# Stored parts in places of their own, a written order for TensorE, and four extra matmuls

## What is computed

```python
Q, K = rope(x @ qw), rope(x @ kw)                 # 16 heads of 8
score = einsum('bhqd,bhkd->bhqk', Q, K) / sqrt(8) - 1e10 * (1 - causal)
weights = softmax(score - max(score))
attn = einsum('bhqk,bhkd->bhqd', weights, V)
x = layernorm(x + merged(attn) @ ow)
gates = top-2 of softmax(x @ router_w + router_b), normalised
h = silu(x @ w1[e]) * (x @ w3[e])
x = layernorm(x + sum_e gates[e] * (h @ w2[e]))
```

## Time and profile before

| what | us |
|---|---|
| median of three runs | 496.91 (495.39 to 498.34) |
| the profiled execution, its time | 497.89 |
| its span, first to last instruction | 496.2 |
| TensorE busy | 416.2 |
| VectorE busy | 313.3 |
| ScalarE busy | 267.1 |
| GpSimd busy | 190.2 |

### The profile page before, as it was taken

One profiled execution on the slowest core, in us unless ns is written; L12 is line 12 of the kernel. 1 busy time (PEld: TensorE's weight loads), 2 busy tenths in 40 slices (PEclk: granted clock), 3 DMA queues, 4 the chain that ended last, 5 costly groups with the idle time before them and its releaser, 6 DMA issues.

```text
span 496.2 us, 7475 instructions
## 1 busy us (share of the span) xinstructions
PE 416.2 (84%) x2397; PEld 209.4 (42%) x2420; DVE 313.3 (63%) x1027; ACT 267.1 (54%) x377; POOL 190.2 (38%) x255
## 2 busy tenths in 40 slices
PE   5715473899898998989989888989999999999992
PEld 2302310222223222232222322327888788788781
DVE  3526374687887878878778786333556756765844
ACT  1220300557556576575755757676665575565560
POOL 3631320205215152151431513224565574665662
PEclk9957555799999999999999999889999999999996
DMA  6644544021122121221212100000000000000000
GB/s 230 190 125 120 159 100 122 13 63 47 20 65 50 47 61 24 65 49 40 60 33 64 41 3 0 3 0 1 2 0 2 21 1 1 22 1 2 22 0 21
DMA packets 46198, 23.47 MB, mean 47 GB/s; under 512 B 30320, under 2 KB 43248, under 8 KB 46160
## 3 DMA queue, kind: packets, MB, share of 16 engines
q1 hardware_dynamic: 46160, 23.00, 17.6%
HBM read 14.21 MB, written 8.59 MB: 46 GB/s over the span
## 4 chain that ended last, share of the span: by engine, by line
PE 58%; DVE 17%; SPq 7%; DMA 6%; ACT 5%; issue 4%; POOL 2%; POOLq 0%; DVEq 0%; ACTq 0%
PE o_bank L1055 12%; PE t_bank L1123 8%; PE bank L1123 8%; PE t_bank L1134 8%; DVE maxima L789 7%; PE t_bank L1038 6%; PE bank L1015 6%; PE small_bank L1015 3%; DMA q_op<-max_rows 3%; SPq L408 3%; DVE mg_w L785 2%; DVE mg_t L785 2%; DVE x_w L785 2%; SPq L367 2%; ACT num L628 2%
## 5 line engine op out<-in xcount | busy, mean ns | idle before, releaser
L628 ACT ACTIVATE num<-t_bank 128x1024 f32<-128x1024 f32 (+2 forms) x160 | 145.1, 939 | 110.1 <-PE t_bank L1038 108.8
L549 POOL TENSOR_TENSOR hid_lo<-num,q_op 128x512 fp32r<-128x512 f32 x64 | 83.0, 1300 | 60.9 <-ACT q_op L684 59.7
L518 POOL TENSOR_SCALAR_AFFINE_SELECT num<-num 128x512 f32<-128x512 f32 x64 | 40.3, 636 | 145.6 <-ACT num L628 145.5
L1015 PE MATMUL bank<-k_op,q_op 128*128 128x512 bf16 (+7 forms) x241 | 74.4, 338 | 22.8 <-DMA k_op<-k_scratch 10.8
L1055 PE MATMUL o_bank<-num,v_op 128*32 128x512 f32 (+3 forms) x768 | 84.5, 513 | 1.1
L1038 PE MATMUL t_bank<-q_op,k_op 64*128 64x512 bf16 (+3 forms) x384 | 59.8, 339 | 11.9 <-DMA q_op<-max_rows 10.2
L684 ACT ACTIVATE q_op<-num 128x512 fp32r<-128x512 f32 x64 | 40.5, 632 | 45.1 <-DVE num L916 44.7
L789 DVE TENSOR_REDUCE maxima<-bank 128x1 f32<-128x512 f32 x85 | 58.4, 688 | 7.9 <-PE bank L1015 4.5
L785 DVE CUSTOM_DVE_ANT_0 mg_t<-bank,resid 128x320 f32<-128x320 f32 (+6 forms) x85 | 37.9, 446 | 23.2 <-PE bank L1015 14.4
L1015 PEld LDWEIGHTS bank<-k_op,q_op 128*128 128x128 bf16 x255 | 23.2, 98 | 67.3 <-DVE maxima L789 20.8
L1038 PEld LDWEIGHTS t_bank<-q_op,k_op 64*128 64x128 bf16 x384 | 16.0, 93 | 76.6 <-issue 46.3
(11 more groups left out here) (132 smaller groups left out, 640.8 us busy)
## 6 DMA issues: line engine op xcount, KB each, us to landing
k_op<-k_scratch SPq DMA_DIRECT2D x32, 128.0 KB, 2.3
q_op<-q_scratch SPq DMA_DIRECT2D x64, 51.0 KB
q_scratch<-rope_part SPq DMA_DIRECT2D x24, 128.0 KB, 2.4
k_scratch<-rope_part SPq DMA_DIRECT2D x24, 128.0 KB, 2.4
w_raw<-in_w_all SPq DMA_DIRECT2D x6, 512.0 KB, 4.1
xT<-in_x_feat SPq DMA_DIRECT2D x4, 256.0 KB, 5.4
k_scratch<-k_op SPq DMA_DIRECT2D x4, 256.0 KB
q_op<-max_rows SPq DMA_DIRECT2D x64, 3.0 KB
```

Source lines behind the costliest of these rows:

```text
L518: pool.affine_select(out=tile, in_=tile, compare_op=ALU.is_ge, fill=0.0, base=0, pattern=[[0, GH], [1, P]], channel_multiplier=-1)\
L549: pool.tensor_tensor(hid_lo[:, m % HB, :], hid[:, m % HB, :], hid_hi[:, m % HB, :].bitcast(F32), ALU.subtract).then_inc(f_lo, 1)
L628: act.activation(num[:, t % PB, :, off:CH].rearrange("p (k i) t -> p i k t", i=2)[:, :, h:h + each, :], t_bank[k % TB][:, :, 0:each * (CH ...
L1015: pe.matmul(ring(s, step)[:, 0:width], q_op[u][:, pr, j, :, :].rearrange("p i q -> p (i q)"), k_op[u][:, pr, lo:lo + width], start=True, s ...
```

## The change

Five things.

1. `rope_part` becomes a view of `num` with a place for each of the eight n. The waits of ScalarE and GpSimd for `parts_stored` go; ScalarE waits for all stores once, before the first exponential.
2. The operand rows are ordered by feature, then product, in DRAM. Each part is stored by one transfer with a broadcast source (three, two or one copy) instead of three, two and one transfers. Which part stands in which row set changes with it (Q_AT, K_AT).
3. The rows of ones stay in SBUF (a memset of the whole k_op), and loads bring 48 rows for each head: `load_k` has four transfers instead of two, `load_q` four of 48 rows, and from group 2 on four more of three zero rows. In the prologue ScalarE issues the first k loads and half of the first q loads. The memset of the second q_op moves behind the last `third_part`, with one of the second k_op.
4. STEADY comes from a string with one letter for each step (s, t, p, m, n) instead of `stage_plan`.
5. WARM = 4 matmuls (fp32, 128 x 512) into t_bank0 stand before the first T, in the prologue's order, with their result overwritten by T.

```diff
+Q_AT = ((2, 5, 1), (1, 6, 4), (0, 1, 1))
+K_AT = ((0, 3, 1), (3, 6, 2), (4, 5, 1))
...
+WARM = 4
...
+STEADY_ORDER = ("ssssstmsstsssttssspsssttnspstsssppsstsstsspsstsspssttsspsmsttsspssttsspsssttpssnttpp")
...
-STEADY = stage_plan(True, True)
+STEADY = steady_plan(STEADY_ORDER)
...
+        def load_q(eng, n, u, c, heads):
+            for h in heads:
+                pr, i = divmod(h, 2)
+                at = (n * GH + h) * DH
+                eng.dma_start(q_op[u][i * HR:i * HR + KROWS, pr, c * NB:(c + 1) * NB, i, :],
+                              q_dram[at:at + DH, :, c * CH:(c + 1) * CH].rearrange("d r t -> (d r) t"))\
+                    .then_inc(q_loaded[u][c], 16)
+                if n > 1:
+                    eng.dma_start(q_op[u][i * HR + KROWS:i * HR + QROWS, pr, c * NB:(c + 1) * NB, i, :],
+                                  z_dram[:, c * CH:(c + 1) * CH]).then_inc(q_loaded[u][c], 16)
...
-                    for r, of in enumerate(K_PART if is_k else Q_PART):
-                        if of == part:
-                            sp.dma_start(dram[heads, r * DH:(r + 1) * DH, cols], rope_part[part][:, n % 2, :])\
-                                .then_inc(parts_stored[n % 2], 16)
+                    sp.dma_start(dram[b * P:(b + 1) * P, first:end:step, c * CH:(c + 1) * CH],
+                                 rope_part[:, n, part, :].unsqueeze(1).broadcast_to([P, copies, CH]))\
+                        .then_inc(parts_stored[ch], 16)
...
-            pool.memset(k_op[0][:, 0, :], 1.0).then_inc(ops_filled, 1)
+            pool.memset(k_op[0][:, :, :], 1.0).then_inc(ops_filled, 1)
...
-                if n == 1:
-                    pool.memset(q_flat[1][:, :].bitcast(F32), 0.0).then_inc(ops_filled, 1)
             for n in range(2 * CHUNKS - 2, 2 * CHUNKS):
                 third_part(n)
+            pool.memset(q_flat[1][:, :].bitcast(F32), 0.0).then_inc(ops_filled, 1)
+            pool.memset(k_op[1][:, :, :], 1.0).then_inc(ops_filled, 1)
...
-                if n >= 2:
-                    act.wait_ge(parts_stored[n % 2], STORES * 16 * (n // 2))
...
+                if n == 4:
+                    act.wait_ge(parts_stored[0], 2 * PARTS * 16)
+                    act.wait_ge(ops_filled, 2)
+                    load_k(act, 0, 0, 0)
+                    load_q(act, 0, 0, 0, range(2, GH))
...
                     if plan is PROLOGUE and step == ("T", 0, 0, 0, 1):
                         pe.wait_ge(v_copied, CHUNKS)
+                        for i in range(WARM):
+                            pe.matmul(t_bank[0][:, i % 2, :], wqk[:, i % 2, :], xT[:, 0:CH], start=True, stop=True)
```

More of the change, by code:

```diff
@@ L148, in stage_plan, with steady_plan @@
     return [(*step, next(uses)) if step[0] in ("MROWS", "NORM") else step for step in plan]
+STEADY_ORDER = ("ssssstmsstsssttssspsssttnspstsssppsstsstsspsstsspssttsspsmsttsspssttsspsssttpssnttpp")
+def steady_plan(order):
+    s_units, small = iter(S_UNITS), iter([("MROWS", NC - 1), ("MROWS", 0)])
+    norms = iter([("NORM", NC - 1), ("NORM", 0)])
+    t_units = iter([(*u, 0) for u in T_UNITS[T_END[0]:]] + [(*u, 1) for u in T_UNITS[:T_END[0]]])
+    tiles, use, plan = iter(T_TILES), iter(range(len(order))), []
+    for letter in order:
+        if letter == "s":
+            plan.append(("S", *next(s_units)))
+        if letter == "t":
+            plan.append(("T", *next(t_units)))
+        if letter == "p":
+            c, kt = next(tiles)
+            plan.append(("PV", c, kt))
+            if kt == TI * (c + 1) - 1:
+                plan.append(("OCOPY", c))
+        if letter == "m":
+            plan.append((*next(small), next(use)))
+        if letter == "n":
+            plan.append((*next(norms), next(use)))
+    return plan + [("END",)]
 PROLOGUE = stage_plan(True, False)
-STEADY = stage_plan(True, True)
+STEADY = steady_plan(STEADY_ORDER)
+assert [sum(x[0] == k for x in STEADY) for k in ("S", "T", "PV", "MROWS", "NORM")] == [NS, NT, NPV, 2, 2]
 LAST = stage_plan(False, True)
@@ L241, in transformer_block @@
         roped = sb("roped", [P, 2, CH])
-        rope_part = [sb(f"rope_part{r}", [P, 2, CH], BF16) for r in range(PARTS)]
         q_flat = [sb(f"q_op{u}", [P, NPR * S], F32R) for u in range(2)]
@@ L336, in _ @@
             sp.wait_ge(ops_filled, 1)
[L337 to L354, removed]
+            sp.dma_start(z_dram, q_op[0][0:PARTS, 0, 0:NB, :, :].rearrange("p j i q -> p (j i q)"))\
+                .then_inc(zeros_stored, 16)
             def store(n):
@@ L359, in store @@
                 b, c = divmod(ch, NC)
-                cols = slice(c * CH, (c + 1) * CH)
-                heads = slice(b * H, (b + 1) * H)
                 dram = k_dram if is_k else q_dram
-                for part in range(PARTS):
+                for part, (first, end, step) in enumerate((Q_AT, K_AT)[is_k]):
+                    copies = len(range(first, end, step))
                     sp.wait_ge(part_ready[part], n + 1)
-                    for r, of in enumerate(K_PART if is_k else Q_PART):
-                        if of == part:
-                            sp.dma_start(dram[heads, r * DH:(r + 1) * DH, cols], rope_part[part][:, n % 2, :])\
-                                .then_inc(parts_stored[n % 2], 16)
@@ L370, in stored @@
[L370 to L375, removed]
-                store(n)
[L377 to L382, removed]
-            load_q(0, 0, 1)
-            load_k(0, 0, 1)
+                    sp.dma_start(dram[b * P:(b + 1) * P, first:end:step, c * CH:(c + 1) * CH],
+                                 rope_part[:, n, part, :].unsqueeze(1).broadcast_to([P, copies, CH]))\
+                        .then_inc(parts_stored[ch], 16)
@@ L385, in _ @@
+            for n in range(3):
+                store(n)
+            sp.wait_ge(parts_stored[0], 2 * PARTS * 16)
+            load_q(sp, 0, 0, 0, range(2))
+            for n in range(3, 2 * NC):
+                store(n)
+            sp.wait_ge(parts_stored[1], 2 * PARTS * 16)
+            load_q(sp, 0, 0, 1, range(GH))
+            load_k(sp, 0, 0, 1)
             for n in range(2 * NC, 2 * CHUNKS):
                 store(n)
-            sp.wait_ge(ops_filled, 3)
+            sp.wait_ge(ops_filled, 4)
@@ L388, in _ @@
             for c in range(NC):
-                load_q(1, 1, c)
-                load_k(1, 1, c)
-            stored(CHUNKS)
+                load_q(sp, 1, 1, c, range(GH))
+                load_k(sp, 1, 1, c)
+            for ch in range(NC, CHUNKS):
+                sp.wait_ge(parts_stored[ch], 2 * PARTS * 16)
+            sp.wait_ge(zeros_stored, 16)
             for dst, src in ((wo[:, :], ow), (rw[:, :], router_w),
@@ L607, in _ @@
             copy_v(3)
+            for ch in range(CHUNKS):
+                act.wait_ge(parts_stored[ch], 2 * PARTS * 16)
             act.sem_inc(t_exped, TB)
```

50 lines of the change are left out of this document (27 added, 23 removed).

## The result

| | median, us | lowest to highest |
|---|---|---|
| before, 4 runs | 497.62 | 495.39 to 498.48 |
| after, 4 runs | 475.39 | 473.82 to 477.02 |

The ratio is 0.956 (95% interval 0.951 to 0.961): faster by 22 us, inside the range of 469 to 494 and 6 us under the forecast of 481.5. The profiled execution took 473.82 with a span of 471.8, so the two profiles differ by 24.4 us of span.

The account below looks back on a forecast made before the run. No engine full; a stage's first part ends on a SyncE-issued DMA, its second loses to late scores. Prologue -8.4, clock -1.3, first stage -2.3, six stages -4.5: -16.5 from 497.89 gives 481.4, stated as 481.5; range 469 to 494.

Parts of the forecast that it names:

- second part: Steady stage from T(1,0), a group's first transposed score, to T(1,7), chunk 1's last: 18.5 us, from 21.04.
- the order gives nothing: Rival for the steady stages: stalls stay, period 33.0 us, time set at 496; chance 0.12.
- First part: Steady stage from T(1,7) to the next T(1,0): 12.0 us, from 10.2; 10.4 in the stage without loads ahead.
- SyncE's block: Twelve transfers SyncE issues after T(1,7), ahead of the max_rows copies: 7.1 us, bounds 6.0 to 9.9.
- second path: After T(1,7): w_raw landing 4.4, w_hi 1.1, exponential 1.0, T and max transpose 0.5, VectorE's copy 0.4 us.
- TensorE waiting for max_rows by 1 to 2 us in each stage but the first: Sign at T(1,0) that the forecast case holds; the wait would be gone in the rival of 471.
- The rival at 471: Engines bound the stage: short block, w_raw in time, first part 10.4, period 28.9 us; chance 0.22.
- The slower rival: SyncE's queue at the stage's end becomes the bound: q loads 1.24, period 34.2, time 502.7 us; chance 0.09.
- Prologue: Before the stages: first transposed score at 77.2 instead of 85.56 us, -8.4, bounds -4 and -13.
- The loop: Prologue: ScalarE's copies, GpSimd's third part and sum pace a chunk at 3.7 us; stalled 4.8 and more.
- SyncE's tail: Prologue: SyncE's queue after the second group's loads, 9.0 us, ending at 73.2 (78.6 with slow q loads).
- No free filler: Prologue: the four extra matmuls delay the start by 4 us over 73.2 and return 1.3 by a higher clock.

Follow-up runs that it names:

- e4: kernel before with only the new STEADY string in place of stage_plan: 480.46 us, ratio 0.963 to the kernel before.
- e3: kernel after with the old STEADY list (stage_plan) put back: 483.26 us, ratio 0.966 to the kernel before.
- e2: kernel after with the w_raw load issued earlier, at T(1,0) behind the q loads: 455.09 us, ratio 0.911 to the kernel before.
- e10: kernel after with w_raw issued ahead of the four k loads instead of behind them: 458.09 us, ratio 0.919 to the kernel before.
- e7: kernel before with only the parts in places of their own, so no waits for stored buffers: 495.20 us, ratio 0.993.
- e5: kernel before with each 51-row q load issued as two, 48 and 3 rows: 488.40 us, ratio 0.979.
- e1: kernel after with WARM = 0, the four extra matmuls left out: 473.19 us, ratio 0.949 to the kernel before.
- e8: kernel after with both w_raw issued at T(1,0) and WARM = 0: 452.36 us, ratio 0.908 to the kernel before.

## Why the prediction was right, point by point

The time lies in the range and the direction was right. The forecast period was met by luck, two misses that cancel; the 6 us beyond the forecast come from the prologue, the first boundary and the clock in the last stage.

**What bounds the kernel** was read rightly: no engine was full, and the stage splits into a part that the order sets and a part that a chain of transfers sets. e4 and e3 confirm that the second part goes with the order alone, to 0.04 us.

**Second part.** Forecast 18.5 from T(1,0) to T(1,7), measured 17.6 on average (17.54 in the first stage, 80.86 to 98.40). The term was mis-sized: I allowed 0.1 us for each of 16 changes of kind and 0.5 of left-over stalls, 0.9 too much together. The sign "VectorE's idle of 0.3 to 0.6 between products gone" came in part: its waits in this part fell from 4.6 to 2.0 us, and single ones are still 0.3 to 0.5. In the table's cut a second part gained 3.2 on average for 2.54 forecast, seven times 0.64 or 4.5 us. The rival "the order gives nothing" is refuted by e4.

**First part: wrong path, and a total 1.0 too short.** Forecast 12.0 from T(1,7), measured 13.0 on average (12.4 to 14.1). The period of 30.6 against 30.5 looks exact, but it is 1.0 too little here and 0.9 too much in the second part: luck. The forecast let SyncE's block set this part (0.4 + 7.1 + 2.96 + 1.2 = 11.7) and called w_raw a second path that "meets it". The block took 4.8, since a 48-row load costs 0.31 where I took 0.60 and a three-row load 0.35 where I took 0.74. The price of a max_rows copy was the wrong neighbour: it writes the same piece, but its source lies in SBUF; the range named the other end (a k load, 0.41), and that was the right one. The second path alone set the part. Its links were named (landing, w_hi, exponential, T, max transpose), and SyncE was to get its work "at 7.4 to 9" after T(1,7): it got it after 7.6 (98.40 to 106.02; 7.1 to 7.9 in the six stages). In e2, where T(1,0) waits for max_rows, it starts 4.1 us after the copies do, which would make this path 11.7 long; in the kernel after it starts 4.6 to 6.5 us after them without a wait, so TensorE's own work, at the lower clock, ends the part. That was in no term. So two errors worked against each other: a block 2.3 too long, and the slower work left out. The latter is about 1.4 a stage, as a rest: e10's first parts are 2.9 shorter (8.03 against 10.97), and TensorE's waits for ScalarE, 14.1 us against 4.9 in six stages, are 1.5 of that. By TensorE's busy time it is 1.0.

So the text's own test "TensorE waiting for max_rows by 1 to 2 us in each stage but the first" failed: after, it waits 0.52 in the first and not in the others, and for ScalarE 2.4 instead. "ScalarE waits for w_raw by more than 3 us" was named as what would make the prediction wrong; it waits 2.9 on average and 3.1 in one stage, so that sign was all but there.

**The rival at 471** (block short, w_raw in time, period 28.9) had the right price for the block and missed the condition on w_raw. e2 meets both conditions and e10 nearly (0.9 of waiting is left), and they go below its period, with 27.2 and 27.6: it also carried the second part's 0.9 too much, and 10.4 for a first part that takes 9.7 in e2 and 9.8 in e3, with the old order. **The slower rival** needed q loads of 1.24; they took 0.31.

**Prologue.** Forecast first T at 77.2, measured 73.89. The loop was right (3.7 forecast, 3.81 measured), the max transpose came at 55.71 instead of 57.9, and the matmuls took 5.22 instead of 7.0, since the clock rose while they ran (0.69 on average over them). Both are sizes, not mechanisms. "More important, ScalarE and GpSimd no longer wait" isn't borne out: alone that is worth 3.3 (e7) and the short loads alone 7.5 (e5), since the queue takes its place; the forecast had SyncE's tail in its sum, but not as the condition for the gain.

**The extra matmuls.** "No free filler" was right: e1 puts their cost at 3.4 (e8 at 2.4), forecast 4. They return 0.7, forecast 1.3. The other 2.3 us between first T and T(1,0) are the order's: e4, with neither matmuls nor new loads, has 7.61 there against 9.94. The forecast counted one boundary without loads, and there are two, ahead of the first steady stage and behind the last.

**Slips in the sums.** The tail of SyncE's queue adds up to 73.0 and not 73.2, and the slow block stands there with 9.7 and with 9.9. Neither changes a case. The 2.7 us that the old order is said to lose have no working; by the text's own sum of 18.0 it is 3.0.

**Last stage and expert phase.** Forecast unchanged but for 0.2, measured 2.7 us shorter (-1.6 and -1.1 in the table). Both go with the clock. Windows of the kernel before and of the kernel after, in each the last first part, then from the last T(1,0) to the T(1,7) behind it:

```profile
305.60:315.47 9.87, 7.83 (x62) 3.89 (x59) 2.69 (x11) 5.86 (x8) 3.13 (x9) 0.83 0.02 3
315.47:332.04 16.57, 14.59 (x113) 4.18 (x110) 7.05 (x29) 14.15 (x19) 2.92 (x4) 0.90 0.00 0
```

```profile
283.97:292.24 8.27, 6.02 (x59) 3.06 (x59) 3.21 (x13) 5.85 (x8) 3.51 (x9) 1.00 0.02 3
292.24:307.51 15.27, 13.14 (x112) 4.20 (x109) 7.06 (x29) 14.03 (x19) 2.82 (x4) 1.00 0.01 2
```

That is 1.6 and 1.3 us for about the same work. In the first window e2 has 0.83 again and e1 and e8 have 1.00; in the second e1 has 0.90 and e10 1.00. So it follows none of the edits, and these 2.7 us are no gain that the change was built for. What decides the clock there stays open.

## What to carry to other kernels

A better order for the bound engine and a longer queue of transfers in one change must be priced at the step where they meet: ask for each prefetch in the queue what now stands ahead of its issue and which engine first reads it, since moving one issue by 1.8 us was worth nearly as much here (17 us) as the whole new order (19). Price a transfer that isn't in the trace by one with the same kind of source and split, not by one with the same destination. A wait that a buffer lifts is worth only what the next one in line, here the queue of stores and loads, leaves of it.

## What the runs showed of the hardware that I had not expected

- A stop of about 2.4 us of TensorE among small matmuls went with a lower granted clock behind it in all six stages (0.75 over the 12 us part, 1.00 without the stop), for 1.0 to 1.4 us more on top of the stop. After stops of 0.6 to 1.0 us (e4) two stages of six had it.
- A three-row load from DRAM holds the queue for 0.35 us, and three rows of the same shape out of SBUF hold it for 0.70 (0.74 from one to the next).
- Splitting a 51-row load into 48 and 3 rows took the queue time for four heads from 3.96 to 2.93 us with one transfer more for each head, and the two k loads behind them from 1.69 to 0.81.
- Four fp32 matmuls ahead of the first scores took 5.22 us, moved these by 2.4 to 3.4 us and bought 0.7 us of faster work.
